# A four-layer mixer network on one core: two small vectors fetched at the start, and the router's top-six search placed behind one chunk of the feed-forward

## The chip, the cores and the metric

The kernel runs on one core of a Trainium2 chip. A core has a matrix engine (TensorE, PE in the profile), a vector engine (VectorE, DVE), a scalar engine (ScalarE, ACT), GpSimd (POOL) and SyncE (SP), which here only issues DMA transfers. The engines run their own instruction streams in order and meet at semaphores. The metric is the device time of the whole program in microseconds, lower being better.

## The reference

`x` is 4 x 256 tokens of 256 features, `ctx` has the same shape. Eight residual steps follow each other, each on a layer norm of `x`:

```python
x = x + _L0_xattn_ref(_layernorm(x), itok, ctx, ctx, ctx)
x = x + _L0_ffn_ref(_layernorm(x), L0_ffn_w1, L0_ffn_w3, L0_ffn_w2)
x = x + _L1_xattn_ref(4, 256, 256, L1_xattn_w, L1_xattn_u, _layernorm(x), ctx)
x = x + _L1_ffn_ref(_layernorm(x), gate_weight, inv_mapping, ...)
x = x + _L2_xattn_ref(...)
x = x + _L2_ffn_ref(...)
x = x + _L3_xattn_ref(...)
x = x + _L3_ffn_ref(...)
```

The third step is the recurrent mixer: a scan over the 256 positions with a decay vector `w` and a bonus vector `u`, 256 values each.

```python
no  = jnp.maximum(o, u + kt);  A  = jnp.exp(o - no);      E  = jnp.exp(u + kt - no)
y   = (A * p + E * vt) / (A * q + E)
no2 = jnp.maximum(w + o, kt);  A2 = jnp.exp(w + o - no2); E2 = jnp.exp(kt - no2)
```

The fourth is a mixture of experts with a shared gated FFN of 352 hidden features beside it. Its router takes, for each token, the six largest of 64 softmax scores:

```python
scores = jax.nn.softmax(x @ gate_weight.T, axis=-1)
topk_w, topk_idx = jax.lax.top_k(scores, 6)
w_dense = zeros((T, 64)).at[arange(T)[:, None], topk_idx].add(topk_w)
flat = w_dense[:, inv_mapping];  scalar = flat.sum(-1);  soft = softmax(where(flat == 0, -1e9, flat))
y  = sum_f scalar[:, f] * expert_f(x, soft[:, f])
sh = silu(h @ sh_gate_W.T) * (h @ sh_up_W.T) @ sh_down_W.T
```

## The kernel before, in words

The program keeps `x` transposed (`x_t`, features on the 128 partitions, two blocks of 128, 1024 tokens) and works on two halves of 512 tokens. The order on each engine is written out by hand, and all steps of the eight layers stand one behind the other in five blocks, one for each engine. Big buffers share one area of on-chip memory, `arena`; what lies at one place changes from layer to layer.

**The loads.** SyncE issues the inputs and the weights of the layers 0 and 1 first, then those of `L2_ffn` and `L3_ffn`. The two vectors of the recurrent mixer come after these, and behind a wait: their place `wk["w"]`, `wk["u"]` is at the start of the arena, where the FFN of layer 0 keeps its own data, so SyncE waits until that FFN has added its result to `x_t` (`x_ready`, twice the number of the norm plus 2). Behind the two comes a wait for `slots_clear`, which GpSimd gives after eight memsets, and then the loads of the first two experts (`load_slot`). Each transfer of the two vectors moves single elements, 128 x 2 of them.

**The recurrent mixer.** VectorE waits for both vectors (`load["wku"]`), clears the first columns of `o`, `p` and `q`, and runs `maxima(0)`, `maxima(1)`, `states`, `denominator`, `numerator`, `quotient` for the first half of the tokens and then for the second, with the exponentials on ScalarE between.

**The shared FFN of layer 1 and the router.** `ffn(l1, ...)` runs three chunks of hidden features for each half of the tokens; the chunks are counted 0 to 5 over both halves (`i` in `between`). For a chunk TensorE makes gate and up products, ScalarE takes silu, VectorE multiplies the two (`gate_std`, its instruction's line is 1962, and it counts up `gated`), and TensorE multiplies the chunk before it by the down weights (`down(i - 1)`), which waits for that chunk's `gated`. The router is spread over the chunks: logits behind chunk 2, its exponential on ScalarE, and then on VectorE the function `top_experts`, which `ffn` calls ahead of the second half: softmax normalisation (lines 1980 to 1983), eight `max` instructions (line 1986), eight `match_replace` (line 1989) and the product `wd` (line 1990), which gives `rt_wd`. TensorE transposes `wd` behind chunk 4 (`weights_turned`, line 939), ScalarE copies it, and TensorE maps it behind chunk 5 (`weights_mapped`). The sequence on TensorE in the second half is so: products of chunk 3, products of chunk 4, `down` of chunk 3, `weights_turned`, products of chunk 5, `down` of chunk 4, `weights_mapped`, `down` of chunk 5. After that VectorE adds the result to `x_t` (line 1698) and makes the gates of the experts.

Of the kernel before, what the change touches and what calls it, by code (L numbers as in the profile page):

```python
# [24 lines left out]
P = 128  # L25
D = 256
KC = D // P
BATCH = 4
SEQ = 256
# [32 lines left out]
def build(nc, a, out, stop=None):  # L62
# [5 lines left out]
    with ExitStack() as ctx:  # L68
        def sb(name, shape, dt=F32):
            return ctx.enter_context(nc.sbuf_tensor(name, shape, dt))  # L70

        def sem(name):
            return ctx.enter_context(nc.semaphore(name))
# [16 lines left out]
        mean_w = sb("mean_w", [P, P])  # L90
        head_mask = sb("head_mask", [P, P])
        eps_col = sb("eps_col", [P, 1])


        with nc.sbuf_tensor("arena", [P, ARENA * 256], F32) as arena:
# [39 lines left out]
        c = Cut(0)  # L135
# [5 lines left out]
        c = Cut(c.at / 256)  # L141
# [6 lines left out]
        c = Cut(0)  # L148
# [4 lines left out]
        c = Cut(ARENA - 24 - 18)  # L153
# [5 lines left out]
        c = Cut(75.5)  # L159
# [23 lines left out]
        c = Cut(45.0625)  # L183

        slots = []
        for _ in range(2):
# [4 lines left out]
                d=c([KC, PACK + P]), dqa=c([PACK + P]), qb=c([P]), qb_rest=c([P]),  # L191
# [4 lines left out]
        def part_weights(b):  # L196
# [5 lines left out]
        tern_tmp2 = Cut(45.0625)([6 * D])  # L202

        c = Cut(0)
        wk = dict(w=c([KC]), u=c([KC]), **{n: c([KC, 2, SEQ + 1]) for n in ("o", "p", "q")},
                  **{n: c([TH, KC, 2, SEQ]) for n in ("e1", "e2", "e3", "e4")})
        assert c.at / 256 <= 45.0625
        c = Cut(0)
# [14 lines left out]
        c = Cut(0)  # L223
# [6 lines left out]
        c = Cut(92)  # L230
# [27 lines left out]
        c = Cut(0)  # L258
# [21 lines left out]
        c = Cut(0)  # L280
# [13 lines left out]
        load = {n: sem("load_" + n) for n in ("ctx", "x", "tid", "l0", "l1", "mu", "wku", "inv", "moe0", "moe1",  # L294
                                               "l2w", "l2x", "l2", "l3x", "bg", "l3")}
        turned, evac_act, evac_dve = sem("turned"), sem("evac_act"), sem("evac_dve")
        weights_fixed = sem("weights_fixed")
        x_ready = sem("x_ready")
# [164 lines left out]
        def std_ffn(name, wts, h):  # L463
            ch = chunks(h)
            return dict(name=name, n=len(ch), rows=[w for _, w in ch],
                        w1=lambda k, i: wts[0][:, k, ch[i][0]:ch[i][0] + ch[i][1]],
                        w3=lambda k, i: wts[1][:, k, ch[i][0]:ch[i][0] + ch[i][1]],
                        w2=lambda i, o: wts[2][0:ch[i][1], i, o * P:(o + 1) * P])
# [5 lines left out]
        l1 = std_ffn("l1", wt_l1, H1)  # L474
# [10 lines left out]
        LN = dict(l0x=0, l0=1, wkv=2, l1=3, l2x=4, l2=5, l3x=6, l3=7)  # L485
# [71 lines left out]
        def _(sp):  # L557
# [17 lines left out]
            for k in range(KC):  # L575
# [2 lines left out]
            sp.dma_start(inv_row[0:NE], a["L1_ffn_inv_mapping"].rearrange("f k -> (f k)").partition_broadcast(NE)  # L578
                         ).then_inc(load["inv"], 16)

            for w, n in zip(w_l2, ("L2_ffn_w1", "L2_ffn_w2", "L2_ffn_w3")):
                rows_in(w, a[n], load["l2"])
            for w, n in zip(w_l3, ("L3_ffn_gate_w", "L3_ffn_up_w", "L3_ffn_down_w")):
# [31 lines left out]
                       a["L1_ffn_down_qb"][f1, :, i * P:(i + 1) * P, :].rearrange("f k p r -> p (f k) r"))  # L615
                go(b["s_down"], a["L1_ffn_down_scale"][f1].rearrange("f (c p) -> p (f c)", p=P), True)


            sp.wait_ge(x_ready, 2 * LN["wkv"] + 2)
            for n, d in (("L1_xattn_w", wk["w"]), ("L1_xattn_u", wk["u"])):  # L620
                sp.dma_start(d, a[n].rearrange("(k p) -> p k", p=P),
                             allow_slow_non_contiguous=True).then_inc(load["wku"], 16)

            sp.wait_ge(slots_clear, 1)
            load_slot(0, 0)
# [7 lines left out]
            with sp.Fori(1, NF // 2) as pair:  # L633
                for s in range(2):
# [8 lines left out]
                             allow_slow_non_contiguous=True).then_inc(load["l2x"], 16)  # L643
            sp.dma_start(att_small["bpp"], a["L2_xattn_bp"].rearrange("(k p) -> p k", p=P),
                             allow_slow_non_contiguous=True).then_inc(load["l2x"], 16)
# [26 lines left out]
            for w, n in zip(lx_nat, ("L3_xattn_Wq", "L3_xattn_Wg", "L3_xattn_Wo", "L3_xattn_Wkv")):  # L672
                rows_in(w, a[n], load["l3x"])
            sp.dma_start(bg, a["L3_xattn_bg"].rearrange("(k p) -> p k", p=P),
                             allow_slow_non_contiguous=True).then_inc(load["bg"], 16)
# [982 lines left out]
        def _(dve):  # L1658
# [57 lines left out]
            def ffn(s, gate, y_scale=None, between=None, lead=None):  # L1716
                at = ln_steps(s["n"])
                for h in range(TH):
                    norm = INSIDE[s["name"]][h]
                    if lead:  # L1720
                        lead(h)
                    for i in range(s["n"]):
                        u = s["u0"] + h * s["n"] + i
                        r = s["rows"][i]
                        dve.wait_ge(act_ready, u + 1)
                        if s["split"] and (h or i >= 2):

                            dve.wait_ge(hid_low, s["v0"] + h * s["n"] + i - 1)
                        elif u >= 2:

                            dve.wait_ge(hid_used, u - 1)
                        gate(h, i, r, act_buf[0:r, u % 2, :], ps[0:r, 2 * (u % 2), :], ps[0:r, 2 * (u % 2) + 1, :],
                             hid_buf[0:r, u % 2, :]).then_inc(gated, 1)
                        if s["split"] and i:
                            hidden_low(s, h, i - 1)
                        if between:
                            between(h * s["n"] + i)
                        if norm and i == at["xc"]:
                            ln_xc_of(*norm)
                        if norm and i == at["diag"]:  # L1740
                            ln_diag_of(*norm)
                        if norm and i == at["xn"]:
                            ln_xn_of(*norm)
                        if norm and i == at["parts"]:
                            ln_low(*norm)
                    if s["split"]:
                        hidden_low(s, h, s["n"] - 1)
                    dve.wait_ge(hid_used, s["u0"] + (h + 1) * s["n"])
                    add_y(h, y_scale).then_inc(x_ready, 1)
# [214 lines left out]
            def norm_and_router(i):  # L1964
                if i == 0:
                    ln_diag_of("l1", 1)
                if i == 1:
                    ln_xn_of("l1", 1)
                if i == 2:
                    dve.wait_ge(rt_logits, 1)  # L1970
                    lg = ps[:, 6, :].rearrange("p (t e) -> p t e", e=NE)
                    step(dve.tensor_reduce(R["mx"], lg, AX.X, ALU.max))
                    step(TTN(R["e"], lg, b3(R["mx"], NE), ALU.subtract))
                    dve.sem_inc(exp_in, 1)

            def top_experts(h):
                if h == 0:
                    return
                dve.wait_ge(exp_out, 1)
                step(dve.tensor_reduce(R["sum"], R["e"], AX.X, ALU.add))  # L1980
                step(dve.reciprocal(R["sum"], R["sum"]))
                step(TTN(R["sc"][:, :, 0:NE], R["e"], b3(R["sum"], NE), ALU.mult))
                step(dve.memset(R["sc"][:, :, NE:NE + 2], -1.0))

                for t in range(TT):
                    step(dve.max(R["top"][:, t, :], R["sc"][:, t, 0:NE]))
                step(dve.memset(R["top"][:, :, TOP:8], -1.0))
                for t in range(TT):
                    step(dve.match_replace(R["mr"][:, t, :], R["top"][:, t, :], R["sc"][:, t, :], -2.0))
                STT(R["wd"], R["mr"][:, :, 0:NE], -2.0, R["sc"][:, :, 0:NE], ALU.is_equal, ALU.mult).then_inc(rt_wd, 1)  # L1990

            ffn(l1, gate_std, None, norm_and_router, top_experts)
            dve.wait_ge(rt_flat, 1)
            fl, fm = (R[n].rearrange("p t (f k) -> p (t f) k", k=NK) for n in ("fl", "fm"))
            step(dve.tensor_copy(R["fl"], ps[:, 6, :].rearrange("p (t e) -> p t e", e=NE)))
# [190 lines left out]
            for n in range(4):  # L2186
                h, k = divmod(n, 2)
# [82 lines left out]
            for h in range(TH):  # L2270
                ln_diag_of("l3", h)
                ln_xn_of("l3", h)
                for k in range(KC):
                    n = 2 * h + k
# [62 lines left out]
```

## Time and profile before

| | us |
|---|---|
| median of 3 runs | 1154.09 (1151.56 to 1157.75) |
| the profiled execution, its own time | 1153.47 |
| its span in the trace | 1151.8 |
| TensorE busy / VectorE / ScalarE | 955.2 / 796.0 / 465.1 |

The span is from the first to the last instruction in the trace; 1.67 us of the profiled execution's time lie around it. The place of the two vectors is at 166 to 170 us of the span, that of the search at 250 to 273 us.

### The profile page before, as it was taken

Reading aid. Unit: us, or ns where it says so; the run is one execution under the profiler, and the core shown is the slowest. Engines: PE = TensorE matmul, PEld = TensorE weight load, DVE = VectorE, ACT = ScalarE, POOL = GpSimd, SP = SyncE. Lnnn points to the kernel's source line nnn. Section 1 sums busy time; section 2 is a strip of 40 time slices with the busy share of each in tenths; the row PEclk is TensorE's granted clock in tenths of the full one; section 3 lists DMA queues with packets and bytes.
Section 4 is the critical chain, followed back from the end, with each engine's and each line's share of the span. In section 5 each row is a group of like instructions: output and inputs, shape, how many; then the busy total and the mean of one; then the engine's idle time right before and its main releaser. Section 6 shows DMA issues by size and latency. Waiting matters only on the chain.

```text
span 1151.8 us, 11946 instructions
## 1 busy us (share of the span) xinstructions
PE 955.2 (83%) x4190; PEld 542.2 (47%) x4190; DVE 796.0 (69%) x1160; ACT 465.1 (40%) x708; POOL 19.0 (2%) x50
## 2 busy tenths in 40 slices
PE   5999874596899999999981889999878988767996
PEld 3445542353555555555460333333445666543565
DVE  2675349854488888886686899998734436566884
ACT  2223336631222232222135889898624343412111
POOL 2000000002000000000100000000000000000000
PEclk8999795597799999999985555555579889858998
DMA  9300003001121111100008988898510000000000
GB/s 279 112 0 1 1 11 51 0 1 37 23 31 30 20 17 25 30 1 1 10 0 158 161 158 145 148 161 146 115 46 1 1 0 1 1 1 0 6 13 18
DMA packets 208725, 56.42 MB, mean 49 GB/s; under 512 B 190414, under 2 KB 207524, under 8 KB 208676
## 3 DMA queue, kind: packets, MB, share of 16 engines
q1 hardware_dynamic: 208676, 55.78, 24.8%
q8 instruction: 29, 0.48, 0.2%
q14 instruction: 20, 0.16, 0.0%
HBM read 20.62 MB, written 1.05 MB: 19 GB/s over the span
## 4 chain that ended last, share of the span: by engine, by line
PE 61%; DVE 25%; ACT 7%; issue 4%; DMA 3%; SPq 0%; DVEq 0%; ACTq 0%
PE ps L763 55%; DVE arena L2166 5%; DMA arena<-xc 2%; PE ps L445 2%; ACT xc L1573 1%; PE ps L893 1%; DVE xn_t L1692 1%; DVE arena L1861 1%; DVE arena L2169 1%; DVE sq L2061 1%; DVE sq L2064 1%; PE ps L1142 1%; DVE xc L1676 1%; ACT sq L1347 1%; PE ps L1265 1%
## 5 line engine op out<-in xcount | busy, mean ns | idle before, releaser
L763 PE MATMUL ps<-arena 128*128 128x16 f16 (+8 forms) x1760 | 319.7, 327 | 57.8 <-DMA arena<-arena 21.7
L763 PE MATMUL ps<-arena_split 128*128 128x512 f32 (+6 forms) x832 | 241.9, 442 | 18.7 <-DVE arena_split L1713 11.4
L763 PEld LDWEIGHTS ps<-arena 128*128 128x128 f16 (+5 forms) x1760 | 133.8, 130 | 216.2 <-issue 160.5
L763 PEld LDWEIGHTS ps<-arena_split 128*128 128x128 f32 (+6 forms) x832 | 162.5, 197 | 87.9 <-issue 34.7
L2166 DVE TENSOR_REDUCE arena<-ps 128x1 f32<-128x1024 f32 x128 | 155.6, 1216 | 20.0 <-PE ps L763 20.0
L1573 ACT ACTIVATE xc<-ps,arena 128x1024 int16<-128x1024 f32 x128 | 153.9, 1203 | 19.4 <-DVE arena L2169 9.4
L763 PE MATMUL ps<-sq,arena 128*64 128x512 f32 (+2 forms) x192 | 93.5, 602 | 4.8 <-DVE sq L2064 4.4
L1504 ACT ACTIVATE xc<-ps 128x512 f32<-128x512 f32 x16 | 9.6, 597 | 155.0 <-PE ps L763 155.0
L1382 ACT ACTIVATE act_buf<-ps 128x512 f32<-128x512 f32 (+2 forms) x34 | 20.3, 597 | 97.5 <-PE ps L763 97.4
L763 PE MATMUL ps<-mean_w,sq 128*128 128x1 f32 x240 | 36.2, 281 | 24.3 <-ACT sq L1347 24.3
L445 PE MATMUL ps<-ident,arena 128*128 128x128 f32 (+4 forms) x194 | 36.1, 335 | 20.3 <-DMA arena<-in_x 6.8
L763 PEld LDWEIGHTS ps<-mean_w,sq 128*128 128x128 f32 x240 | 36.4, 237 | 31.1 <-ACT sq L1347 29.2
L763 PEld LDWEIGHTS ps<-sq,arena 128*64 128x64 f32 (+2 forms) x192 | 29.0, 171 | 43.3 <-issue 30.0
L763 PE MATMUL ps<-x_t,mean_w 128*128 128x512 f32 x64 | 38.5, 734 | 11.8 <-DVE x_t L1883 5.9
L445 PEld LDWEIGHTS ps<-ident,arena 128*128 128x128 f32 (+4 forms) x194 | 27.2, 171 | 33.8 <-issue 12.4
L763 PE MATMUL ps<-rsd_diag,ones 128*128 128x512 f32 x32 | 24.3, 850 | 22.1 <-DVE rsd_diag L1686 22.0
L1962 DVE TENSOR_TENSOR hid_buf<-ps,act_buf 128x512 f32<-128x512 f32 (+2 forms) x18 | 12.3, 689 | 42.7 <-ACT act_buf L1382 42.7
L763 PE MATMUL ps<-xn_t,arena 128*128 128x256 f32 (+2 forms) x112 | 36.4, 475 | 2.7 <-DVEq L2228 2.7
L1347 ACT ACTIVATE sq<-xc 128x1024 f32<-128x1024 f32 x15 | 15.8, 1050 | 52.5 <-DVE xc L1676 52.5
L763 PE MATMUL ps<-xn_t,ctx_t 128*128 128x512 f32 x64 | 32.4, 636 | 1.4 <-DVE xn_t L1692 1.4
L763 PE MATMUL ps<-hid_buf,ctx_t 128*128 128x512 f32 x64 | 30.5, 599 | 1.4 <-DVE hid_buf L1833 1.4
L1676 DVE TENSOR_TENSOR xc<-x_t,ps 128x1024 f32<-128x1024 f32 x16 | 19.5, 1217 | 16.1 <-PE ps L763 16.0
(274 smaller groups left out, 1230.8 us busy)
## 6 DMA issues: line engine op xcount, KB each, us to landing
arena<-in_L_ffn_w SPq DMA_DIRECT2D x4, 640.0 KB, 5.0
arena<-xc SPq DMA_TRANSPOSE x112, 3.3
arena<-in_x SPq DMA_DIRECT2D x1, 1024.0 KB, 5.8
arena<-in_ctx SPq DMA_DIRECT2D x1, 1024.0 KB, 8.5
arena<-in_L_ffn_gate_w SPq DMA_DIRECT2D x1, 1024.0 KB, 10.0
arena<-in_L_ffn_up_w SPq DMA_DIRECT2D x1, 1024.0 KB, 12.4
arena<-in_L_ffn_down_w SPq DMA_DIRECT2D x1, 1024.0 KB, 12.0
arena<-in_L_ffn_gate_W SPq DMA_DIRECT2D x8, 128.0 KB, 2.0
```

The lines of the kernel that those rows point to most:

```text
L445: last = pe.transpose(ps[0:m, 6 + g % 2, col:col + w], src, ident[0:src.shape[0], 0:src.shape[0]])
L763: return pe.matmul(o, l, r, start=start, stop=stop)
L893: return pe.transpose(ps[0:m, bank, col:col + n], src, ident[0:n, 0:n])
L1142: last = pe.transpose(ps[:, 7, :].bitcast(BF16)[:, k * P:(k + 1) * P], y[:, k * P:(k + 1) * P], ident_b[:, :])
L1265: last = pe.transpose(ps[:, 2 * h + k, j * P:(j + 1) * P], src[:, k, t * P:(t + 1) * P], ident[:, :])
L1347: act.activation(ln_sq_tile(name, h), xc[:, h], ACT.Square).then_inc(ln_sq, 1)
L1382: act.activation(act_buf[0:r, u % 2, :], ps[0:r, 2 * (u % 2), :], func, scale=1.0 if scale is None else scale[0:r, :]).then_inc(act_ready, 1)
L1573: act.activation(att_y[:, u % 4, :].rearrange("p (a b) -> p a b", a=2), ps[:, score_banks(u), :], ACT.Exp, bias=att_small["bias"][:, u % 3 ...
L1676: TTN(xc[:, h], x_t[:, :, tok(h)], ps[:, b:b + 1, :].to_broadcast([P, KC, HALF]), ALU.subtract).then_inc(ln_xc, 1)
L1692: TTN(xn_t[:, :, tok(h)], xc[:, h], ps[:, b:b + 1, :].to_broadcast([P, KC, HALF]), ALU.mult).then_inc(xn_ready, 1)
L1962: return TTN(hid, up, s, ALU.mult)
L2166: dve.tensor_reduce(A["nm"][:, b:b + 1], ps[:, score_banks(u), :], AX.XY, ALU.max, negate=True).then_inc(att_max, 1)
```

## The change

The two vectors get a buffer of their own, `wku`, outside the arena, and SyncE issues their transfers without a wait, behind the small loads of layer 1 and ahead of the weights of `L2_ffn` and `L3_ffn`. The scan's buffers keep their order in the arena and move up by the four words per partition that are left. `top_experts` is cut into two: `shares` (the softmax) stays where the whole was, and `chosen` (the search) is called behind VectorE's product of chunk 3.

```diff
+        wku = sb("wku", [P, 2, KC])
...
-        wk = dict(w=c([KC]), u=c([KC]), **{n: c([KC, 2, SEQ + 1]) for n in ("o", "p", "q")},
+        wk = dict(w=wku[:, 0, :], u=wku[:, 1, :], **{n: c([KC, 2, SEQ + 1]) for n in ("o", "p", "q")},
...
+            for n, d in (("L1_xattn_w", wk["w"]), ("L1_xattn_u", wk["u"])):
+                sp.dma_start(d, a[n].rearrange("(k p) -> p k", p=P),
+                             allow_slow_non_contiguous=True).then_inc(load["wku"], 16)
             for w, n in zip(w_l2, ("L2_ffn_w1", "L2_ffn_w2", "L2_ffn_w3")):
                 rows_in(w, a[n], load["l2"])
...
-            sp.wait_ge(x_ready, 2 * LN["wkv"] + 2)
-            for n, d in (("L1_xattn_w", wk["w"]), ("L1_xattn_u", wk["u"])):
-                sp.dma_start(d, a[n].rearrange("(k p) -> p k", p=P),
-                             allow_slow_non_contiguous=True).then_inc(load["wku"], 16)
 
             sp.wait_ge(slots_clear, 1)
             load_slot(0, 0)
...
                     dve.sem_inc(exp_in, 1)
-
-            def top_experts(h):
+                if i == 3:
+                    chosen()
+
+            def shares(h):
                 if h == 0:
                     return
                 dve.wait_ge(exp_out, 1)
...
                 step(dve.memset(R["sc"][:, :, NE:NE + 2], -1.0))
 
+            def chosen():
                 for t in range(TT):
                     step(dve.max(R["top"][:, t, :], R["sc"][:, t, 0:NE]))
...
-            ffn(l1, gate_std, None, norm_and_router, top_experts)
+            ffn(l1, gate_std, None, norm_and_router, shares)
```

On SyncE's queue of transfers, in the stretch from the last small loads to the first load of an expert, this stands before (`arena<-in_L_xattn_w` and `_u` are the two vectors, `in_L_ffn_inv_mapping` the last small load):

```order
L578 DMA arena<-in_L_ffn_inv_mapping 64x64
...
L566 DMA arena<-in_L_ffn_gate_w 128x8x256
L566 DMA arena<-in_L_ffn_up_w 128x8x256
L566 DMA arena<-in_L_ffn_down_w 128x2x1024
L621 DMA arena<-in_L_xattn_w 128x2x1
L621 DMA arena<-in_L_xattn_u 128x2x1
L593 DMA arena<-in_L_ffn_gate_W 128x256
```

and this of the change:

```order
L579 DMA arena<-in_L_ffn_inv_mapping 64x64
L583 DMA wku<-in_L_xattn_w 128x2x1
L583 DMA wku<-in_L_xattn_u 128x2x1
...
L567 DMA arena<-in_L_ffn_gate_w 128x8x256
L567 DMA arena<-in_L_ffn_up_w 128x8x256
L567 DMA arena<-in_L_ffn_down_w 128x2x1024
L597 DMA arena<-in_L_ffn_gate_W 128x256
```

The two transfers have moved ahead of eight bigger ones, and no wait for layer 0 stands before them.

On VectorE, from the end of the first half's chunks in the shared FFN to the end of the second half's, this stands before (`MAX` and `MATCH_REPLACE` are the search, the rows that read `ps` and `act_buf` the chunks' products):

```order
L1698 TENSOR_TENSOR x_t<-ps,x_t 128x2x512
L1980 TENSOR_REDUCE arena<-arena 128x8
L1981 RECIPROCAL arena<-arena 128x8
L1982 TENSOR_TENSOR arena<-arena 128x8x64
L1983 MEMSET arena 128x8x2
L1986 MAX arena<-arena 128x8 x8
L1987 MEMSET arena 128x8x2
L1989 MATCH_REPLACE arena<-arena 128x66 x8
L1990 SCALAR_TENSOR_TENSOR arena<-arena 128x512
L1962 TENSOR_TENSOR hid_buf<-ps,act_buf 128x512 x2
L1962 TENSOR_TENSOR hid_buf<-ps,act_buf 96x512
```

and this of the change:

```order
L1697 TENSOR_TENSOR x_t<-ps,x_t 128x2x512
L1981 TENSOR_REDUCE arena<-arena 128x8
L1982 RECIPROCAL arena<-arena 128x8
L1983 TENSOR_TENSOR arena<-arena 128x8x64
L1984 MEMSET arena 128x8x2
L1961 TENSOR_TENSOR hid_buf<-ps,act_buf 128x512
L1988 MAX arena<-arena 128x8 x8
L1989 MEMSET arena 128x8x2
L1991 MATCH_REPLACE arena<-arena 128x66 x8
L1992 SCALAR_TENSOR_TENSOR arena<-arena 128x512
L1961 TENSOR_TENSOR hid_buf<-ps,act_buf 128x512
L1961 TENSOR_TENSOR hid_buf<-ps,act_buf 96x512
```

One product, that of chunk 3, has moved ahead of the search's eighteen instructions; the other engines' orders are the same in both programs, SyncE's apart.

## Rows read from the trace of the kernel before

**Rows 1.** The page's part 4: engines' shares of the chain that ended last.

```profile
PE 61%; DVE 25%; ACT 7%; issue 4%; DMA 3%; SPq 0%; DVEq 0%; ACTq 0%
```

**Rows 2.** Windows: busy us (instructions) of each engine, clock, DMA.

```profile
core 0: us, PE busy (x) PEld busy (x) DVE busy (x) ACT busy (x) POOL busy (x), PEclk, DMA share, GB/s
...
170.40:223.60 53.20, 19.89 (x62) 13.06 (x62) 51.52 (x65) 36.32 (x47) 0.00 (x0) 0.56 0.21 30
```

**Rows 3.** Timeline of VectorE, 165 to 171 us: start, us, instruction, [idle before].

```profile
165.16 1.23 DVE L1698 TENSOR_TENSOR x_t<-ps,x_t 128x1024 f32<-128x1024 f32 x1 [1.29 <-PE ps L763]
170.38 0.06 DVE L1886 MEMSET arena<- 128x4 f32 x1 [3.99 <-DMA arena<-in_L_xattn_u]
```

**Rows 4.** Timeline of SyncE, 166 to 192 us.

```profile
166.82 0.48 SPq L621 DMA_DIRECT2D arena<-in_L_xattn_u  x1
...
168.76 0.84 SPq L593 DMA_DIRECT2D arena<-in_L_ffn_gate_W  x2
...
191.16 0.58 SPq L593 DMA_DIRECT2D arena<-in_L_ffn_down_scale  x1
```

**Rows 5.** Timeline of VectorE, 228 to 229 us: the first expert's scales.

```profile
228.81 0.41 DVE L1916 TENSOR_SCALAR arena<-arena 128x64 f32<-128x64 f32 x2
```

**Rows 6.** Timeline of SyncE, 17 to 31 us.

```profile
17.32 3.18 SPq L578 DMA_DIRECT2D arena<-in_L_ffn_inv_mapping  x1
...
27.05 3.62 SPq L566 DMA_DIRECT2D arena<-in_L_ffn_down_w  x1
```

**Rows 7.** Timeline of VectorE and GpSimd, 280 to 285 us.

```profile
280.62 0.69 DVE L2006 TENSOR_TENSOR arena<-arena 128x512 f32<-128x512 f32 x1
280.69 1.64 POOL L747 TENSOR_TENSOR arena<-arena 1x512 f32<-1x512 f32 x1
...
283.74 1.15 POOL L750 TENSOR_TENSOR arena<-arena 1x512 f32<-1x512 f32 x1
```

**Rows 8.** Timeline of VectorE, 252 to 273 us (x8, x2: merged).

```profile
252.58 2.06 DVE L1986 MAX8 arena<-arena 128x8 f32<-128x64 f32 x8
...
257.41 0.69 DVE L1990 SCALAR_TENSOR_TENSOR arena<-arena 128x512 f32<-128x512 f32 x1
258.02 1.28 DVE L1962 TENSOR_TENSOR hid_buf<-ps,act_buf 128x512 f32<-128x512 f32 x2
...
272.33 1.22 DVE L1698 TENSOR_TENSOR x_t<-ps,x_t 128x1024 f32<-128x1024 f32 x1 [4.25 <-PE ps L763]
```

**Rows 9.** Timeline of TensorE, 249 to 268 us.

```profile
249.42 7.03 PE L763 MATMUL ps<-xn_t,arena 128*128 128x512 f32 x16
258.76 3.67 PE L763 MATMUL ps<-hid_buf,arena 128*128 128x512 f32 x4 [2.31 <-DVE hid_buf L1962]
262.27 1.04 PE L939 MATMUL ps<-ident,arena 128*64 128x128 f32 x8
...
266.58 1.88 PE L763 MATMUL ps<-hid_buf,arena 128*128 128x512 f32 x4
```

**Rows 10.** Timeline of ScalarE, 253 us.

```profile
253.06 0.60 ACT L1382 ACTIVATE act_buf<-ps 128x512 f32<-128x512 f32 x1 [1.77 <-PE ps L763]
```

**Rows 11.** Windows around the search: busy us of each engine, clock.

```profile
250.80:258.10 7.30, 5.65 (x14) 2.19 (x12) 6.50 (x32) 1.68 (x3) 0.00 (x0) 1.00 0.00 0
258.10:262.27 4.17, 3.51 (x4) 1.35 (x5) 1.20 (x3) 0.00 (x0) 0.00 (x0) 0.59 0.00 0
262.27:272.33 10.06, 10.06 (x43) 5.60 (x41) 0.69 (x1) 1.61 (x2) 0.00 (x0) 1.00 0.00 1
```

**Rows 12.** Timeline of TensorE: two other pauses.

```profile
60.01 0.36 PE L763 MATMUL ps<-arena,ones 128*128 128x6 f32 x2 [1.65 <-DVE xn_t L1692]
...
938.43 2.07 PE L763 MATMUL ps<-rsd_diag,ones 128*128 128x512 f32 x2 [1.61 <-DVE rsd_diag L1686]
```

**Rows 13.** Windows, TensorE alone, behind these two pauses.

```profile
59.90:63.30 3.40, 3.29 (x9) 1.00 0.00 0
...
938.30:941.20 2.90, 2.77 (x5) 0.50 0.00 0
```

## The prediction

> **What bounds the kernel now.** I read the page first: the chain that ended last is mostly TensorE and VectorE, in turns [rows 1]. So there is no single bound, and each stage has to be asked for the wait that ends last in it. The chain by order of time shows the two stages that the diff touches: the recurrent mixer, in which every step is VectorE's, and the shared FFN with the router, in which the chain goes from TensorE to VectorE for the search and back. A table of windows confirms the first: in the 53.2 us of the mixer VectorE is busy for 51.52 us [rows 2]. What delays its start there delays the end by as much. For the rest I read the timeline of each engine in these two places. The reader is to see two holes: VectorE idle for 3.99 us before its first memset of the mixer, released by the transfer of `u` [rows 3], and TensorE idle for 2.31 us before the down product of chunk 3, released by VectorE's product, with these four passes taking 3.67 us behind it [rows 9].
>
> **Part A, the two vectors.** Before, VectorE ends the addition to `x_t` at 166.39, SyncE may issue only then (`u` at 166.82), and the memset starts at 170.38 [rows 3, 4]. With both vectors landed long before, the memset can start where the hole begins: -4.0 us. Nothing else may release it later: its input `xn_t` is VectorE's own work, and the buffers it clears belong to that FFN, whose last read came before the addition. Behind it the stage is a row of VectorE instructions with 1.7 us of holes in 53.2 us [rows 2], so I count the 4.0 whole.
>
> What was moved: two transfers. SyncE's issues at the start run from 17.32 (the last small load) to 30.67 (the last weight of layer 3) [rows 6]; two issues more, of at most 0.48 us each by the row of `u` [rows 4], make the eight that follow about 0.9 us later. These weights are needed by layers 2 and 3 and by no step before 200 us, so this costs nothing; without that cover it would be 0.9 us. At the old place two issues fall away, but the experts' loads there do not start earlier, since their own wait, GpSimd's memsets, ended at 168.76 [rows 4]. That stays put while VectorE comes 4 us nearer to them: the last load of the two is issued at 191.16, and the first scales are used at 228.81, in future at 224.8 [rows 4, 5]. Over 30 us of cover are left.
>
> New is that GpSimd's memsets, which lay in VectorE's hole (both begin at the addition's end, and SyncE's next issue at 168.76 waits for their end [rows 4]), now lie under VectorE's first scans. The nearest row is a `tensor_tensor` of VectorE under one of GpSimd: VectorE's took 0.69 us, as its others of this size do, and GpSimd's took 1.64 us where the same instruction later took 1.15 [rows 7]. So GpSimd pays and VectorE does not. I take 0; the bound on the bad side is that VectorE waits for the whole of the memsets, 168.76 - 166.39 = 2.4 us. On this the Trainium skill ("SBUF — State Buffer", Who interferes with whom) says that VectorE's instructions with two inputs in SBUF contend with GpSimd instructions that read SBUF, not with those that only write it, and that of two that contend the later one is fully blocked. By that rule memsets and scans do not meet at all, and the price is 0 as well; the case against the change would be a GpSimd copy in their place, with the 2.4 us.
>
> **Part B, the search behind chunk 3.** No instruction is added or removed. Three times move.
> 1. VectorE is ready for the search at 252.58 [rows 8]. Chunk 3's silu runs from 253.06 to 253.66 on ScalarE [rows 10], so VectorE now waits for it, multiplies for 0.69 us, half of the merged pair of rows 8, and starts the search at about 254.35: 1.8 us later. The search ends at 257.41 + 0.69 = 258.10 before, and at 259.9 now. That is the cost, and it is on the path, since the transposes of `wd` need it.
> 2. TensorE has the products of chunks 3 and 4 behind it at 249.42 + 7.03 = 256.45 [rows 9]. Before, it then waited for chunk 3's product, which stood behind the search, began `down` of it at 258.76, at the lower clock (0.59 in this stretch [rows 11]), and reached the transposes at 262.27. Now the product is ready at 254.4, so `down` follows without a pause at the full clock: four passes as in the later row of 1.88 us [rows 9], that is 256.3 to 258.0.
> 3. The transposes start when both are done, at 259.9 instead of 262.27: -2.35 us. From their start to the addition at 272.33 it is 10.06 us of unbroken TensorE work at clock 1.00 [rows 11], the same in both. Chunk 4's product now ends at about 260.6, and its `down` stands behind the transposes and eight passes; it is not late.
>
> TensorE's pause is not gone but moved: from 258.0 to 259.9, 1.9 us instead of 2.31. Behind the old one the clock stood at half (1.2 GHz), which made 3.67 - 1.88 = 1.8 us of the 3.67. Whether it falls behind a pause of this size the trace tells both ways: behind one of 1.65 us it stayed at 1.00 (2.4 GHz), behind one of 1.61 us it went to 0.50 [rows 12, 13]. If it falls, the transposes and the first of chunk 5's passes take what `down` took too long before, 1.8 us, and part B is worth 2.35 - 1.8 = 0.55. So B lies between -0.55 and -2.35. I take -1.6, near the middle, since the rows speak for either about equally.
>
> **The sum.** -4.0 - 1.6 = -5.6 us. The profiled execution took 1153.47 with a span of 1151.8; it becomes 1147.9. The median of the runs is 0.6 above that execution, so I forecast 1148.5 for the median. Measured against 1154.09, half a per cent, about what a measurement of this kernel can tell, is 5.8 us: the forecast lies just inside it, and the verdict hangs on the clock.
>
> **The rivals.**
> - *The clock is kept in the new pause.* Then B is -2.35, the sum -6.35, the median 1147.7. For it: the pause of 1.65 us; against it: that of 1.61. Together with its opposite, *the clock falls again*, sum -4.55, median 1149.5, this is the spread of the forecast; I give the two and what lies between 0.80.
> - *The fetch's gain is partly taken by another wait.* GpSimd's memsets hold VectorE for up to 2.4 us: the sum is -5.6 + 2.4 = -3.2, the median 1150.9. Against it stands rows 7. Chance 0.09.
> - *The change does only one of its two things.* If the router's path is set by something else, part B gives 0 and the sum is -4.0, median 1150.1; if part A's wait is replaced in full by another (a transfer that is late in spite of all, a memset's buffer), only B is left: 1152.5. Against the first: the chain itself goes from the search through `down` to the transposes. Chance 0.07 for both.
> - *Slower.* The search now lies under TensorE's pause as a whole, and the clock, once down, may stay down: if it stayed at half through the whole of the 10.06 us that follow [rows 11], these would take 20.1, and the sum is -4.0 - 2.35 + 10.06 = +3.7, median 1157.8. It decides from about 6.4 us of full-clock work done at the lower clock. Against it: before, the clock was down behind the longer pause of 2.31 us and back at 1.00 in the window from 262.27 [rows 11]. Chance 0.04, a part of it beyond half a per cent.
>
> **The range.** The three cases around the forecast reach from 1147.7 to 1149.5; the runs of one kernel, 1151.56 to 1157.75, lie up to 3 us off their median, and the median of a few runs may lie 2 off. 1147.7 - 2.2 gives 1145.5. Above, the range takes in the contended fetch and one part alone with gain, 1150.9 and 1152.5: 1152.8. Faster by over 0.5% (below 1148.3): a little under half of the forecast's 0.80 and little of the others, plus scatter, 0.46. Within 0.5%: 0.51. Slower: 0.03.
>
> **What would show it.** Part A: no idle time before VectorE's memset behind the addition, the memset within 0.1 us of the addition's end, the first two scans as long as those of the second half of the tokens, which no memset meets, and the same 53.2 us from there to the end of the mixer. Part B: the addition of the second half's result behind that of the first by 0.55 to 2.35 us less than before, VectorE idle for about 1.2 us before chunk 3's product, `down` of chunk 3 at 0.43 us for a pass, directly behind chunk 4's products, and a pause of about 1.9 us before the transposes. Wrong it would be if the first scans were longer than the later ones, if `down` still waited, or if the distance from the transposes to the addition were far above 10.06 us. Everything behind the addition at 272.33 should keep its length; a difference there would be neither of the two parts, but the clock in other stages, which a shift of the work in time may move either way.

## The result and the profile after

| | before | the change |
|---|---|---|
| median of six runs, us | 1155.6 (1151.56 to 1157.75) | 1149.66 (1146.15 to 1150.76) |
| the profiled execution, us | 1153.47 | 1150.76 |
| its span, us | 1151.8 | 1149.1 |

The ratio of the runs is 0.994, with a 95% interval of 0.992 to 0.9959: 5.9 us less between the medians, where 5.6 was forecast. The forecast median was 1148.5; with more runs the kernel before came out at 1155.6 rather than the 1154.09 that the forecast started from, and that is most of the 1.2 us between 1148.5 and 1149.66. The two profiled executions differ by only 2.7 us; why that is less is answered below.

Part A. The timeline of the changed kernel, all engines, in the place of [rows 3, 4] (weight loads and rows between are left out):

```profile
166.06 1.23 DVE L1697 TENSOR_TENSOR x_t<-ps,x_t 128x1024 f32<-128x1024 f32 x1 [2.16 <-PE ps L762]
167.24 0.06 DVE L1885 MEMSET arena<- 128x4 f32 x1
...
167.35 0.32 POOL L734 MEMSET arena<- 128x256 f32 x1 [157.44 <-DVE x_t L1697]
...
167.61 1.42 DVE L1846 TENSOR_TENSOR_SCAN arena<-wku,xn_t 128x256 f32<-128x256 f32 x2
...
169.67 0.82 SPq L597 DMA_DIRECT2D arena<-in_L_ffn_gate_W  x2
```

The bracket behind the memset is gone: it starts 1.18 us behind the start of the addition, where it was 5.22. GpSimd's memsets now run under the scans, and the pair of scans takes 1.42 us all the same. SyncE's first load of an expert again comes behind the memsets, 3.61 us behind the addition's start where it was 3.60.

Part B. VectorE's timeline, in the place of [rows 8]:

```profile
249.56 0.07 DVE L1984 MEMSET arena<- 128x16 f32 x1
250.83 0.69 DVE L1961 TENSOR_TENSOR hid_buf<-ps,act_buf 128x512 f32<-128x512 f32 x1 [1.20 <-issue]
251.44 2.06 DVE L1988 MAX8 arena<-arena 128x8 f32<-128x64 f32 x8
...
256.27 0.69 DVE L1992 SCALAR_TENSOR_TENSOR arena<-arena 128x512 f32<-128x512 f32 x1
256.88 0.68 DVE L1961 TENSOR_TENSOR hid_buf<-ps,act_buf 128x512 f32<-128x512 f32 x1
...
267.10 1.23 DVE L1697 TENSOR_TENSOR x_t<-ps,x_t 128x1024 f32<-128x1024 f32 x1 [4.24 <-PE ps L762]
```

and TensorE's, in the place of [rows 9]:

```profile
246.51 7.03 PE L762 MATMUL ps<-xn_t,arena 128*128 128x512 f32 x16
253.38 1.88 PE L762 MATMUL ps<-hid_buf,arena 128*128 128x512 f32 x4
257.01 1.06 PE L938 MATMUL ps<-ident,arena 128*64 128x128 f32 x8 [1.75 <-DVE arena L1992]
```

VectorE is idle for 1.20 us, until ScalarE's silu ends at 250.75, multiplies, and searches. On TensorE `down` of chunk 3 follows the products without a pause, and its four passes take 1.88 us instead of 3.67; the pause stands ahead of the transposes and is 1.75 us long. The windows of the changed kernel (columns as in [rows 11]) say what the clock did:

```profile
253.38:257.01 3.63, 1.88 (x5) 0.57 (x3) 3.25 (x20) 0.60 (x1) 0.00 (x0) 1.00 0.00 0
257.01:267.10 10.09, 10.09 (x42) 5.62 (x42) 1.24 (x2) 1.61 (x2) 0.00 (x0) 1.00 0.00 1
```

It stayed at 1.00 (2.4 GHz) through the pause, and from the transposes to the addition it is 10.09 us, as before. From the first half's addition to the second's it is 267.10 - 246.71 = 20.39 us, where it was 272.33 - 249.62 = 22.71.

### The profile page after: what moved, and what is told of

Its sections match the earlier page's. It is cut to its first block, busy times and chain, and to the rows that moved or that the text cites. A ratio compares the mean times of both kernels' runs of the same rounds, so it can differ in the third digit from the quotient of the medians.

```text
span 1149.1 us, 11946 instructions
## 1 busy us (share of the span) xinstructions
PE 957.0 (83%) x4190; PEld 546.5 (48%) x4190; DVE 797.1 (69%) x1160; ACT 464.9 (40%) x708; POOL 18.9 (2%) x50
## 3 DMA queue, kind: packets, MB, share of 16 engines
HBM read 20.62 MB, written 1.05 MB: 19 GB/s over the span
## 4 chain that ended last, share of the span: by engine, by line
PE 62%; DVE 25%; ACT 6%; issue 4%; DMA 3%; SPq 0%; DVEq 0%; ACTq 0%
PE ps L762 56%; DVE arena L2168 5%; DMA arena<-xc 2%; PE ps L446 2%; ACT xc L1572 1%; PE ps L892 1%; DVE xn_t L1691 1%; DVE arena L1860 1%; DVE arena L2171 1%; DVE sq L2063 1%; DVE sq L2066 1%; PE ps L1141 1%; DVE xc L1675 1%; ACT sq L1346 1%; PE ps L1310 1%
## 5 line engine op out<-in xcount | busy, mean ns | idle before, releaser
L762 PE MATMUL ps<-arena_split 128*128 128x512 f32 (+6 forms) x832 | 246.5, 449 | 19.0 <-DVE arena_split L1712 11.4
L762 PEld LDWEIGHTS ps<-arena_split 128*128 128x128 f32 (+6 forms) x832 | 165.5, 201 | 89.3 <-issue 34.9
L2171 DVE TENSOR_SCALAR arena<-arena 128x1 f32<-128x1 f32 x128 | 27.4, 214 | 4.5
```

The source lines that it names most:

```text
L762: return pe.matmul(o, l, r, start=start, stop=stop)
L2171: TS(A["bias"][:, b:b + 1], A["nm"][:, b:b + 1], A["sq"][:, t, i:i + 1], math.log(255.0), ALU.mult, ALU.add).then_inc(att_bias, 1)
```

## The experiments

All times are ratios to the kernel before on the same chip. "Between the additions" is the time from the start of the first half's addition to that of the second half's in the shared FFN, the measure of part B.

**One part alone.** The fetch alone has the change's loads and the search back in its old place:

```diff
-                if i == 3:
-                    chosen()
...
                 step(dve.memset(R["sc"][:, :, NE:NE + 2], -1.0))
+                chosen()
```

> The change with the search put back ahead of chunk 3's product, so that part A alone is left. Theory (part A is VectorE's hole of 3.99 us and nothing else): 4.0 us below the kernel before, ratio 0.9965; in the trace the first memset follows the addition within 0.1 us, and the search's stretch is as before, 22.7 us from the start of the first half's addition to that of the second. Rival (the whole gain is part A's, through something in the early loads as well): about 5.9 us below, ratio 0.995 or less. Rival (another wait takes the place): less than 2 us.

Measured: 0.9965, interval 0.9947 to 0.9983, 12 runs: 4.0 us. The memset starts 1.17 us behind the addition's start (165.95 against 164.78), and it is 22.71 us between the additions, as in the kernel before. Its TensorE timeline shows the old picture, clock included:

```profile
254.63 3.51 PE L762 MATMUL ps<-hid_buf,arena 128*128 128x512 f32 x4 [2.31 <-DVE hid_buf L1961]
```

The search alone is the changed kernel with buffer and fetch put back:

```diff
-        wku = sb("wku", [P, 2, KC])
...
+        wk = dict(w=c([KC]), u=c([KC]), ...
...
-            for n, d in (("L1_xattn_w", wk["w"]), ("L1_xattn_u", wk["u"])): ...
...
+            sp.wait_ge(x_ready, 2 * LN["wkv"] + 2)
+            for n, d in (("L1_xattn_w", wk["w"]), ("L1_xattn_u", wk["u"])): ...
```

> The kernel before with the search behind chunk 3's product, and the vectors fetched as before. Theory: between 0.55 and 2.35 us below the kernel before, by whether TensorE's clock is kept over the pause of 1.9 us, ratio 0.998 to 0.9995; together with the fetch alone the two add up to the change's 5.9 us within 1.5 us. Rival (the down product was not on the path): 0. Rival (the search 1.8 us later costs more than down gives back): slower by up to 1.8.

Measured: 0.9982, interval 0.9961 to 1.0003, 12 runs: 2.1 us, by itself not clear of no change. The trace is clearer than the time: VectorE idle for 4.07 us before the memset, 20.39 us between the additions. The two ratios together give 1 - 0.0035 - 0.0018 = 0.9947; the change has 0.994.

**The home without the early fetch.** The vectors lie in `wku`, but are fetched at the old place.

```diff
-            for n, d in (("L1_xattn_w", wk["w"]), ("L1_xattn_u", wk["u"])): ...
...
+            sp.wait_ge(x_ready, 2 * LN["wkv"] + 2)
+            for n, d in (("L1_xattn_w", wk["w"]), ("L1_xattn_u", wk["u"])): ...
             sp.wait_ge(slots_clear, 1)
```

> The changed kernel with the vectors in their own buffer, but fetched at the old place, behind layer 0's FFN. Theory (the home only allows the early fetch, and brings nothing by itself): VectorE idle for 4.0 us before the first memset again, 5.2 us from the addition's start to it; with the search moved, 20.4 us between the additions. Rival (the scans gain or lose by the buffers' new places): the mixer from the memset on is not 48.3 us long up to the next anchor but differs by over 0.2.

One profiled execution. VectorE's timeline of it:

```profile
172.60 0.06 DVE L1887 MEMSET arena<- 128x4 f32 x1 [3.98 <-DMA wku<-in_L_xattn_u]
```

The hole is back, and it is 20.39 us between the additions. From the memset to the first addition it is 79.38 us, against 79.24 before and 79.47 in the change, so the buffers' new places cost nothing that can be seen. The buffer matters only because nothing else lives in it.

**The clock in the pause.** How much of part B is order, and how much the clock? Two spare products that the result does not use fill TensorE's pause, in the kernel before ahead of chunk 3's `down`, in the changed one ahead of the transposes:

```diff
+                        if name == "l1" and h and i == 1:
+                            for _ in range(2):
+                                mm(ps[:, 7, :], mean_w[:, :], xn_t[:, 0, 0:HALF], True, True)
                         if i >= lag:
                             down(i - lag)
```

> The kernel before with the same two spare products in the pause ahead of chunk 3's down. Theory (of part B's 2.35 us in the profiled executions 1.8 are the lower clock behind the pause and 0.55 are order): down takes 1.9 instead of 3.7 us, the addition of the second half's result comes 20.9 us behind the first's instead of 22.7, and the time is about 1.8 us below the kernel before if its clock falls there in every run, less if only in some. Rival (the low clock there is not due to the pause): down still takes 3.7 us, 22.7 us between the additions.

> The changed kernel with two spare products of 128x512 (four passes, 1.7 us at full clock) in TensorE's pause ahead of the transposes; they add work that the result does not use. If the clock falls behind the pause in some runs, this takes it away: the same time or up to 1 us less on the mean, the addition of the second half's result 20.4 us behind the first's or up to 0.1 later. If the pause never cost anything: the same within the scatter.

The kernel before, filled; TensorE's timeline:

```profile
254.39 1.88 PE L763 MATMUL ps<-xn_t,mean_w 128*128 128x512 f32 x4
256.86 1.98 PE L763 MATMUL ps<-hid_buf,arena 128*128 128x512 f32 x4 [0.59 <-DVE hid_buf L1965]
```

`down` takes 1.98 us, and it is 21.02 us between the additions (247.72 to 268.74). So of the 2.32 us between 22.71 and 20.39, 1.69 are the lower clock behind the pause and 0.63 are order. The times do not show these 1.7 us: the ratio is 0.9998, and its interval, 0.9975 to 1.0022, holds both no change and 1.7 us less (0.9985). The changed kernel, filled, is at 20.39 like the unfilled one, and at 0.9955 (0.9928 to 0.9983) against the change's 0.994: nothing to be had there, as the clock had not fallen.

**Is it chance?** The kernel before ran twice more for a trace, the changed one once more with times.

> The kernel before once more, for a second trace. Theory (a pause of 2.3 us in TensorE's work at this place lets the clock fall in most executions, 1.75 us does not): 22.7 us between the additions, down of chunk 3 at 3.7 us. Rival (it falls at random, in the first trace and in that of the fetch alone by chance): 21.0 to 21.3 us between them. The rest differs from the first trace by up to 3 us in the stages behind.

> The same once more, for the same question: 22.7 us between the additions by the theory, 21.0 to 21.3 where the clock is kept.

> The changed kernel once more, for a second trace of it and a time on the same chip as the three below. The two places: first memset 0 to 0.1 us behind the addition, 20.4 us between the additions if the clock is kept in the pause, up to 22.2 if it falls. Theory on the profiled pair's small difference (2.7 us of span where the medians differ by 5.9): the stages behind the search differ between executions of any kernel by the clock, so that the stretch from the second addition to the end is 879 to 885 us here, not the 882.0 of the first trace. Rival (the change lengthens the later stages by 2.5 us): 882 again and no execution of it near 879.

TensorE's row of `down` in the two further traces of the kernel before:

```profile
261.31 3.63 PE L763 MATMUL ps<-hid_buf,arena 128*128 128x512 f32 x4 [2.31 <-DVE hid_buf L1962]
```

```profile
257.86 3.66 PE L763 MATMUL ps<-hid_buf,arena 128*128 128x512 f32 x4 [2.31 <-DVE hid_buf L1962]
```

With the old order the clock was down behind the pause of 2.31 us in four traces of four (three of the kernel before, one of the fetch alone). With the new order it stayed up through 1.75 us in five of five (two of the change, the search alone, the home without the fetch, and GpSimd's copies below). The two orders differ in more than the length of the pause: the old one stands ahead of `down`, the new one ahead of the transposes. No run has the longer pause in the new place or the shorter one in the old.

The changed kernel's second set of times gave 0.9932, interval 0.9908 to 0.9956. In its second trace the memset starts 1.17 us behind the addition's start, and it is 20.39 us between the additions. From the second addition to the end it is 884.6 us, inside the 879 to 885 of the theory, but no trace of this kernel lies near 879. What follows from that is said in point 4 below.

**GpSimd under VectorE.** Two of the four memsets of each slot become copies that read on-chip memory.

```diff
-                step(pool.memset(b["qb_rest"], 0.0))
-                step(pool.memset(b["dqa"], 0.0))
+                step(pool.tensor_copy(b["qb_rest"], b["rest"][:, 0:P]))
+                step(pool.tensor_copy(b["dqa"], b["rest"][:, 0:PACK + P]))
```

> The changed kernel with two of the four memsets of each slot turned into GpSimd copies that read on-chip memory; the result is the same. Part A's bad bound was that GpSimd holds VectorE's scans. Theory (VectorE is not held by GpSimd): the scans stay at 0.7 us each, and GpSimd's copies take longer than the memsets. Rival (the one that comes later is blocked for the whole of the other, as the Trainium skill has it for two that both read): a scan or a two-input instruction of VectorE under a copy takes 0.2 to 0.4 us longer, and the mixer ends up to 1 us later.

VectorE's and GpSimd's timelines of it (one execution):

```profile
167.50 1.42 DVE L1846 TENSOR_TENSOR_SCAN arena<-wku,xn_t 128x256 f32<-128x256 f32 x2
...
169.63 0.75 DVE L1850 SCALAR_TENSOR_TENSOR arena<-xn_t,wku,arena 128x512 f32<-128x512 f32 x1
170.29 1.50 DVE L1846 TENSOR_TENSOR_SCAN arena<-wku,xn_t 128x256 f32<-128x256 f32 x2
```

```profile
167.62 0.66 POOL L735 COPY arena<-arena 128x128 f32<-128x128 f32 x1
168.34 0.77 POOL L736 COPY arena<-arena 128x240 f32<-128x240 f32 x1
...
169.70 0.82 POOL L735 COPY arena<-arena 128x128 f32<-128x128 f32 x1
170.59 0.67 POOL L736 COPY arena<-arena 128x240 f32<-128x240 f32 x1
```

The copies do lie under VectorE's work, and take 0.66 to 0.82 us where the memsets took 0.21 and 0.30. VectorE pays 0.09 us on one pair of scans (1.50 against 1.41 in the change) and nothing on the `SCALAR_TENSOR_TENSOR` instructions between, which keep their 0.75 us. SyncE's first load of an expert comes 1.9 us later (5.52 us behind the addition's start), which its cover hides. In this place the choice between memset and copy is worth nothing on VectorE's path. Two `tensor_tensor` instructions do meet, as the last experiment shows.

**A next step: the transposes behind chunk 5.** After the change TensorE pauses for 1.75 us with chunk 5's products ready to run. This version runs them and chunk 4's `down` first, and maps behind the last `down`:

```diff
-                if i == 4:
-                    weights_turned()
                 if i == 5:
-                    weights_mapped()
+                    weights_turned()
             ffn(l1, norm_and_router)
+            weights_mapped()
...
-                if i == 4:
+                if i == 5:
                     act.wait_ge(rt_wdt, 1)
```

> A next step on the changed kernel: TensorE runs chunk 5's products and chunk 4's down ahead of the transposes of wd, and maps behind chunk 5's down; ScalarE copies wd behind chunk 5's silu. Theory (what is left of the search on the path is TensorE's pause of 1.75 us and the mapping ahead of the last down): no pause ahead of the transposes, the second addition 18.3 to 18.8 us behind the first instead of 20.4, and the router's first copy on VectorE 2 to 3 us earlier; 0.002 below the changed kernel, ratio to before 0.992 to 0.993. Rival (the mapping, now last, waits for ScalarE's copy and sets the end): the same time as the changed kernel.

Measured: 0.9917, interval 0.9886 to 0.9949. TensorE's timeline:

```profile
252.73 1.88 PE L762 MATMUL ps<-hid_buf,arena 128*128 128x512 f32 x4
254.44 3.60 PE L762 MATMUL ps<-xn_t,arena 128*96 128x512 f32 x8
257.88 1.88 PE L762 MATMUL ps<-hid_buf,arena 128*128 128x512 f32 x4
259.60 1.04 PE L938 MATMUL ps<-ident,arena 128*64 128x128 f32 x8
260.47 1.88 PE L762 MATMUL ps<-hid_buf,arena 96*128 96x512 f32 x4
262.28 2.00 PE L762 MATMUL ps<-arena 64*128 64x64 f32 x16
```

There is no pause, and it is 16.33 us between the additions. That is 4.06 less than the change, more than the 1.6 to 2.1 that I expected: I had counted the pause, and not that the mapping's 1.9 us leave the path to the addition and run under it. The two make most of the 4.06. The router's own chain gains less: its first copy on VectorE starts 18.25 us behind the first addition (264.31), where it was 21.53, so 3.28. In the change the mapping was done 18.45 us behind the first addition, and the copy stood behind VectorE's second addition; now it waits for the mapping, which ends no more than 0.2 us sooner. The time, 0.0015 below the 0.9932 of the change on that chip, has an interval that overlaps the change's.

**The search in two pieces.** Four `max` go into VectorE's hole ahead of the product:

```diff
                 step(dve.memset(R["sc"][:, :, NE:NE + 2], -1.0))
+                for t in range(TT // 2):
+                    step(dve.max(R["top"][:, t, :], R["sc"][:, t, 0:NE]))
...
             def chosen():
-                for t in range(TT):
+                for t in range(TT // 2, TT):
```

> The changed kernel with four of the eight max instructions ahead of chunk 3's product, in VectorE's hole of 1.2 us. Theory (the search's end sets the transposes): the transposes start 1.0 us earlier, 19.4 us between the additions, 1.0 us below the changed kernel, too little for the times and to be read from the trace. Rival (chunk 3's product is late by it): 20.4 or more.

It is 19.34 us between the additions, 1.05 less, and TensorE's pause is 0.71 us: the end of the search sets the transposes, as expected. The time is 0.9923, interval 0.9898 to 0.9947, not to be told from the change's 0.9932 on that chip.

**GpSimd's subtraction behind the gates.** In the change's trace, behind the search, an instruction of VectorE takes longer than in any trace of the kernel before (0.69 to 0.70 us there). The two engines' timeline there:

```profile
275.27 1.14 POOL L746 TENSOR_TENSOR arena<-arena 1x512 f32<-1x512 f32 x1
275.40 1.57 DVE L2008 TENSOR_TENSOR arena<-arena 128x512 f32<-128x512 f32 x1
```

In the second trace of the same kernel VectorE came first, and GpSimd's instruction is the long one:

```profile
273.24 0.69 DVE L2008 TENSOR_TENSOR arena<-arena 128x512 f32<-128x512 f32 x1
273.39 1.54 POOL L746 TENSOR_TENSOR arena<-arena 1x512 f32<-1x512 f32 x1
```

The two meet in 13 of the 14 traces. In ten VectorE starts first and takes 0.69 to 0.72 us, GpSimd 1.47 to 1.68; in three GpSimd starts first and takes 1.14, VectorE 1.17 to 1.63. In all 13 the later one ends 1.69 to 1.72 us behind the start of the earlier.

The last version, the fourteenth trace, adds to the one with the transposes behind chunk 5 a wait on GpSimd ahead of that subtraction:

```diff
             step(pool.tensor_copy(bias_parts[0:1], bias_row))
+            pool.wait_ge(rt_gt, 1)
```

> The kernel with the transposes behind chunk 5, and one wait more: GpSimd's subtraction of the bias rows waits until VectorE has written the experts' gates. In some traces VectorE's last product of the gates takes 1.2 to 1.6 us instead of 0.69, where GpSimd's subtraction had started just ahead of it. Theory (the two share a read path, the one that starts later waits): VectorE's product takes 0.69 us, GpSimd's subtraction 1.14, and the time is 0 to 0.5 us below the version without the wait, too little for the times: ratio to before 0.991 to 0.993. Rival (the long product comes from something else): it is still 1.2 us or more in this trace.

```profile
272.19 0.69 DVE L2008 TENSOR_TENSOR arena<-arena 128x512 f32<-128x512 f32 x1
...
273.04 1.14 POOL L747 TENSOR_TENSOR arena<-arena 1x512 f32<-1x512 f32 x1 [1.62 <-DVE arena L2008]
```

Both have their short time. Measured: 0.9892, interval 0.9857 to 0.9927, median 1144.45 against 1157.24: the fastest version of the study, though its interval overlaps that of the version without the wait. What the wait alone brings the times do not tell. In the traces VectorE's next addition (L2013, L2012 without the wait) starts 29.17 us behind the first half's addition with it and 29.66 without, 0.49 us less, at the upper end of what was expected.

## Why the forecast was right, and where it was not

1. *Part A, 4.0 us.* Shown. In the changed kernel the memset is 4.04 us nearer to the addition (1.18 against 5.22), and the fetch alone gives 4.0 us of time. The earlier issues cost nothing that the traces show: the first of the eight weight loads behind them is issued 0.28 us later (20.82 against 20.54), not 0.9, and the last issue ends earlier (29.17 against 30.67). Layer 0's last addition starts at 163.2 to 166.2 us in the eight traces with the early fetch and at 162.4 to 167.5 in the six without. The mixer from the memset on is nearly as long as before: 79.47 us to the first addition in the shared FFN against 79.24.

2. *Part B, 0.55 to 2.35 us, taken at 1.6.* The order of events came as worked out: the product waits for the silu, the search ends later, `down` moves ahead of the pause. The term that was mis-sized is the clock: I put its price between nothing and 1.8 us in the new pause and took 0.7; the runs show nothing in five of five traces, so part B is worth 2.32 us, the upper end of the range that was worked out (2.35). The two pauses of [rows 12], one kept and one lost, made the case look even; here it was not, and why it was not is open. The split, 1.69 us for the clock and 0.63 for the order, is shown in the traces by the filled kernel, not in its time.

3. *GpSimd under the scans, taken at 0.* The size was right and the general reading of [rows 7] was wrong. I concluded that GpSimd pays and VectorE does not. VectorE had started 0.07 us ahead there. (The two GpSimd rows there are two subtractions of one size, L747 and L750, not one instruction twice; the comparison holds.) Where GpSimd starts ahead, as at 275.27 against 275.40 above, VectorE's product takes 1.57 us instead of 0.69: it ends 0.56 us behind the end of GpSimd's. The Trainium skill ("SBUF — State Buffer", Who interferes with whom) calls the port pair that VectorE and GpSimd share an exclusive lock, and says that the order of issue decides who blocks; I had applied it to the memsets alone. Here the 13 traces agree. For memsets it has no meeting, and the scans' 1.42 us agree with it too. For GpSimd's copies it would have VectorE's two-input instructions and the copies block each other, and only 0.09 us of that came on VectorE: there the measurement decides, and the reason is open.

4. *The sum.* The two parts measure 4.04 + 2.32 = 6.4 us in the traces, and the times say 5.9, with 4.7 to 9.2 as the ends of the first set's interval (0.9959 and 0.992 of 1155.6). The profiled pair differs by 2.7. By stages: up to layer 0's last addition the changed execution is 0.90 us later (166.06 against 165.16), at the memset it has gained 4.04, from there to the first addition it loses 0.23, between the additions it gains 2.32, and from the second addition to the end it takes 1149.1 - 267.10 = 882.0 us where the other took 1151.8 - 272.33 = 879.5, 2.53 more: 0.90 - 4.04 + 0.23 - 2.32 + 2.53 = -2.70. Of the last term 0.88 is VectorE's long product. The rest is not the change's code, which is the same there. The same stretch took 876.2 and 882.8 us in the two other traces of the kernel before, 884.6 in the second of the change, and 881.8 to 885.1 with one part alone or the home alone.

Against the medians the profiled pair is an unlucky one: the execution of the kernel before took 2.1 us less than its median, that of the change 1.1 more than its own, the slowest of its six. Where the scatter lies can be read too: between the first and the last addition of the experts' results (320.96 to 567.52 before) all fourteen traces take 246.5 to 246.7 us, while from there to the first addition of layer 2's FFN (890.69) they take 323.2 to 328.6. One stage shows the clock at work. From a cast of VectorE (846.75 us) into layer 2's FFN (its product at 894.77), TensorE alone (length, busy us, clock), first the kernel before, then the change:

```profile
846.70:894.80 48.10, 38.48 (x149) 0.79 0.00 1
```

```profile
844.10:895.30 51.20, 41.85 (x148) 0.71 0.00 1
```

The same work, 3.1 us apart, with the mean clock at 0.79 and 0.71; the search alone has 51.90 us with 0.70. That these executions differ there by the clock is shown. Does a kernel that reaches these stages 6 us earlier lose there in every execution? The traces alone lean that way (876.2 to 882.8 us in the three of the kernel before, 881.2 to 885.1 in the nine others with the same code there), but the times speak against a loss of the profiled pair's size: with 2.5 us lost each time the change would gain 3.8 us, a ratio of 0.9967, and that lies outside both intervals of the change (0.992 to 0.9959 and 0.9908 to 0.9956). A smaller loss stays possible.

The rivals: *the clock is kept* is what happened in the pause. *The fetch's gain is partly taken by another wait* fell, by the scans' 1.42 us and the 4.0 us of the fetch alone. *Only one of the two things* fell by the two experiments with one part alone. *Slower* fell with the clock at 1.00.

## What to carry to other kernels

A small transfer that waits only because its place is in use costs its whole latency, here 4 us: a few words of memory of its own take it off the path. Where one engine has a long serial piece of work, put ahead of it the short instruction that another engine waits for, even if the long piece then ends later, and then ask what else the waiting engine could run in the pause that is left: that second step gave 4.1 us between the additions (3.3 on the router's own chain) where the first gave 2.3. And most of what a reorder is worth may be the clock: of the 2.32 us here 1.69 were the low clock behind the old pause. Whether a pause costs the clock has to be read from the granted clock of the window behind it, in more than one trace.

## What the runs showed of the hardware

- A pause of 2.31 us in dense TensorE work was followed by half the clock (0.51 to 0.55 over the four passes behind it) in four traces of four. One of 1.75 us, in another place of the order, was not in five of five, and elsewhere in the same kernel one of 1.61 us was [rows 12, 13]. The length of the pause alone does not decide.
- A VectorE `tensor_tensor` of 128x512 and a GpSimd one of 1x512, both with two inputs on chip, run one behind the other: in 13 traces of 13 the later one ended 1.69 to 1.72 us behind the start of the earlier. VectorE's went from 0.69 to as much as 1.63 us, GpSimd's from 1.14 to as much as 1.68, by who started first. GpSimd's copies and VectorE's scans did not meet so: 0.09 us in one trace.
- Executions of one kernel differ by about 1% (1138.34 to 1146.78 us for the last version, 1148.28 to 1161.3 for 35 runs of the kernel before). Over these 35 the time goes against the mean granted clock (correlation -0.68; 0.824 in the fastest run, 0.815 in the slowest), and in the traces compared here one stage of layer 2 took 48.10 us at a mean clock of 0.79 and 51.20 at 0.71. A gain of 2 us is therefore seen in the trace of its stage long before it is seen in the times.
